# A two-block token-routed FFN: the second layer of block 1 token-major, two experts side by side, x1 turned feature-major by VectorE blocks and an HBM scratch

## The reference

```python
def block_1(h, ids):                       # h = layernorm(x), ctx is Wg, Wu and Wd
    for e in range(4):
        z = h @ ctx[e].T
        y = (silu(z) * z) @ ctx[e].T       # g and u are the same product
        out = where(expert_of(ids) == e, y, out)
x1 = x + block_1(layernorm(x), ids)

def block_2(h):
    scores = sigmoid(h @ router_w.T)
    combine = normalised scores of the 4 best of scores + e_bias, else 0
    routed = sum over e of combine[:, e] * ((silu(h @ gate[e].T) * (h @ up[e].T)) @ down[e].T)
    return routed + shared_expert(h)
out = x1 + block_2(layernorm(x1))
```

## Time and profile before

| | us |
|---|---|
| median of 3 runs | 173.52 (173.36 to 174.03) |
| the profiled execution | 173.89 |
| its span | 171.8 |
| PE busy | 166.6 (97%) |
| DVE busy | 114.2 (66%) |
| ACT busy | 67.8 (39%) |
| POOL busy | 39.6 (23%) |
| TensorE clock granted | 1.0 (2.4 GHz) |

### The profile page before, as it was taken

How to read it: one execution, slowest core, us unless ns; L and a number is a source line. 1 busy time by engine, 2 the same in 40 slices (tenths; PEclk the granted TensorE clock), 3 DMA queues, 4 the chain that set the end, 5 groups by cost and what they waited for, 6 DMA issues and landing times.

```text
span 171.8 us, 2194 instructions
## 1 busy us (share of the span) xinstructions
PE 166.6 (97%) x728; PEld 130.6 (76%) x728; DVE 114.2 (66%) x230; ACT 67.8 (39%) x112; POOL 39.6 (23%) x37
## 2 busy tenths in 40 slices
PE   6989999999999999999999999999999999999992
PEld 2568888888877888788787778788787887878881
DVE  0779778888984988588688528964744444444452
ACT  2472520551258254824664593152212222223320
POOL 2593000698200025539385000000000000000000
PEclk9999999999999999999999999999999999999999
DMA  4999000176400036742111200043361211100003
GB/s 137 307 373 352 23 4 2 25 236 227 122 0 4 15 130 181 203 160 67 61 61 61 61 0 4 8 126 126 113 195 45 75 65 61 62 0 4 2 0 122
DMA packets 7971, 16.41 MB, mean 95 GB/s; under 512 B 1336, under 2 KB 2200, under 8 KB 7832
## 3 DMA queue, kind: packets, MB, share of 16 engines
q1 hardware_dynamic: 7960, 16.27, 29.0%
HBM read 15.08 MB, written 1.18 MB: 95 GB/s over the span
## 4 chain that ended last, share of the span: by engine, by line
PE 97%; ACT 0%; POOL 0%; DVE 0%; issue 0%; DVEq 0%; POOLq 0%
PE bank L853 26%; PE bank L913 14%; PE bank L911 13%; PE bank L912 13%; PE bank L931 7%; PE bank L934 7%; PE bank L932 7%; PE bank L943 4%; PE bank L820 2%; PE bank L907 1%; PE bank L908 1%; PE bank L832 1%; ACT xn_hi L433 0%; POOL warm L383 0%; DVE xt L732 0%
## 5 line engine op out<-in xcount | busy, mean ns | idle before, releaser
L913 PE MATMUL bank<-xn_lo,gu_hi 128*128 128x512 f32 (+1 forms) x104 | 41.0, 394 | 0.0
L911 PE MATMUL bank<-xn_hi,gu_lo 128*128 128x512 f32 x96 | 37.9, 395 | 0.0
L912 PE MATMUL bank<-xn_hi,gu_hi 128*128 128x512 f32 x96 | 37.8, 394 | 0.0
L501 ACT ACTIVATE h_hi<-hid 128x512 fp32r<-128x512 f32 (+1 forms) x26 | 16.4, 632 | 45.7 <-DVE hid L720 45.7
L725 DVE TENSOR_TENSOR h_lo<-hid,h_hi 128x512 fp32r<-128x512 f32 (+1 forms) x26 | 20.2, 778 | 15.6 <-ACT h_hi L501 15.6
L913 PEld LDWEIGHTS bank<-xn_lo,gu_hi 128*128 128x128 f32 (+1 forms) x104 | 19.4, 186 | 5.0
L491 ACT ACTIVATE act_sb<-bank 128x512 f32<-128x512 f32 (+1 forms) x26 | 15.4, 594 | 18.1 <-PE bank L913 18.0
L398 POOL TENSOR_TENSOR gu_lo<-stage,gu_hi 128x512 fp32r<-128x512 f32 x12 | 17.9, 1516 | 17.6 <-ACT gu_hi L426 17.6
L912 PEld LDWEIGHTS bank<-xn_hi,gu_hi 128*128 128x128 f32 x96 | 18.0, 187 | 4.4
L911 PEld LDWEIGHTS bank<-xn_hi,gu_lo 128*128 128x128 f32 x96 | 18.0, 187 | 4.4
L931 PE MATMUL bank<-h_hi,wd_lo 128*128 128x512 f32 (+1 forms) x52 | 20.6, 396 | 0.0
(11 more groups left out here) (76 smaller groups left out, 213.1 us busy)
## 6 DMA issues: line engine op xcount, KB each, us to landing
stage<-gu_d SPq DMA_DIRECT2D x6, 512.0 KB, 3.5
stage<-wd_d SPq DMA_DIRECT2D x3, 512.0 KB, 4.1
x<-comb_d SPq DMA_DIRECT2D x8, 192.0 KB, 2.7
ids<-comb_d SPq DMA_DIRECT2D x8, 192.0 KB, 3.0
stage<-ctx_d SPq DMA_DIRECT2D x4, 256.0 KB, 5.0
xt<-xt_d SPq DMA_DIRECT2D x1, 1024.0 KB, 10.3
x<-comb_d SPq DMA_DIRECT2D x8, 128.0 KB, 3.1
ids<-comb_d SPq DMA_DIRECT2D x8, 128.0 KB, 2.8
```

What stands on the lines that cost most here:

```text
L911: nc.tensor.matmul(out[:], gu_lo[:, cols], xn_hi[:, h, k], start=(k == 0), stop=False)
L912: nc.tensor.matmul(out[:], gu_hi[:, cols], xn_hi[:, h, k], start=False, stop=False)
L913: ins = nc.tensor.matmul(out[0:rows, :], gu_hi[:, wide], xn_lo[:, h, k], start=False, stop=(k == KC - 1))
```

## The change

**Layer 1 stays as it was**: four mixes of 24 matmuls, now numbered 0 to 3. **Layer 2 becomes eight tiles** of 128 tokens: the tokens' hidden rows are now the stationary operand, two experts' matrices side by side (2 x 256 columns) the moving one, so a tile is two banks of six matmuls. `first_z` and three picks of 128x256 (mask `owned`, one value for a partition, broadcast over the row) choose the expert, and x1 is added in `x`, token-major. The order on PE is mix 0, mix 1, mix 2, tiles 0 to 3, mix 3 (with the norm's transposes after its third expert), gate and up of item 0, tiles 4 to 7.

**Gone**: the 1 MB load of `xt`, both groups of x1 transposes on PE, ACT's copies of x1 (`copy_x1`), `add_block_1`.

**x1 feature-major for the output** is made in two steps. At the end of g = 5 and g = 11 (`X1_TURNS`) DVE turns 32x32 blocks of the half's four tiles from `x` into `xt` (`turn_x1`, four instructions). SP then writes them to the scratch `x1_d` in HBM in eight DMAs (`write_x1`) and, one item later, reads them back in one (`read_x1`). The host orders the tokens of `x` and of the ids to suit; the norm's second transposes write PSUM in runs of 32 columns.

**The norm of x1, first half**, is made in two groups of two tiles (`NORM_GROUPS`), each with its own power on POOL; DVE takes tiles 0 and 2. The spread buffers lie in `ids` and `ctx_lo` now. On ACT the high parts of pieces 4 and 5 stand ahead of `silu_z(2)`.

```diff
-        mixes = [(1, 0, 0), (1, 0, 1), (1, 1, 0), (2, 0, 0), (2, 0, 1), (1, 1, 1), (2, 1, 0), (2, 1, 1)]
+        mixes = [(0, 0), (0, 1), (1, 0), (1, 1)]
+        units = [("mix", 0), ("mix", 1), ("mix", 2)] + [("tile", j) for j in range(TT)]
+        units += [("mix", 3)] + [("tile", j) for j in range(TT, HALVES * TT)]
...
+            def tile(j, masked):
+
+                u = ("tile", j)
+                z = prod[:, turn[u] % 2, 0:D]
+                dve.wait_ge(z_first, turn[u] + 1)
+                dve.wait_ge(dstep, masked)
+                for e in range(1, E1):
+                    dve.wait_ge(z_done, z_at[u, e // 2])
+                    if e > 1:
+                        dve.wait_ge(z_picked, picks_of(u, e - 1))
+                    nc.vector.copy_predicated(z, owned[:, e - 1, j:j + 1].to_broadcast([P, D]),
+                                              ring_bank(u, e // 2)[:, e % 2 * D:(e % 2 + 1) * D]).then_inc(z_picked, 1)
+                dve.wait_ge(z_picked, picks_of(u, E1 - 1))
+                nc.vector.tensor_tensor(x[:, j], z, x[:, j], ALU.add).then_inc(x1_done, 1)
+
+            def turn_x1(h):
+
+                for t in range(TT):
+                    nc.vector.transpose(x1_blocks[h][:, t], x[:, h * TT + t].rearrange("p (b i) -> p b i", i=LANES)).then_inc(x1_turned, 1)
...
+            def write_x1(h):
+                sp.wait_ge(x1_turned, (h + 1) * TT)
+                by_block = x1_d[h].rearrange("(b j) (q c) -> b q j c", b=BLOCKS, c=P)
+                blocks = xt[:, h].rearrange("p k c -> p (k c)")
+                for b in range(BLOCKS):
+                    sp.dma_start(by_block[b], blocks[:, b * P:(b + 1) * P]).then_inc(x1_out, 16)
+
+            def read_x1(h):
+                sp.wait_ge(x1_out, (h + 1) * BLOCKS * 16)
+                sp.dma_start(xt[:, h], x1_d[h].rearrange("(k f) c -> f k c", k=KC)).then_inc(xt_in, 16)
...
+                if g in X1_TURNS:
+                    write_x1(X1_TURNS.index(g))
+                if g - 1 in X1_TURNS:
+                    read_x1(X1_TURNS.index(g - 1))
...
-            first_z(2)
-            silu_z(2)
-            first_z(3)
+            first_z(("mix", 2))
             high_part(4)
             high_part(5)
+            silu_z(2)
...
-            rstd_of(2, 4)
+            rstd_of(3)
+            low_part(E1 + 2)
+            low_part(E1 + 3)
+            rstd_of(4)
...
+            def tile(j):
+
+                u = ("tile", j)
+                h, t = j // TT, j % TT
+                tokens = slice(t * P, (t + 1) * P)
+                for pair in range(E1 // 2):
+                    wait_ring_read(pe, u, pair)
+                    z = ring_bank(u, pair)[:]
+                    experts = slice(2 * pair, 2 * pair + 2)
+                    for k in range(KC):
+                        b = h * KC + k
+                        pe.wait_ge(h1_high, b + 1)
+                        nc.tensor.matmul(z, h_hi[:, b, tokens], ctx_hi[:, experts, k], start=(k == 0), stop=False)
```

More of the change, by code:

```diff
@@ L195, in build @@
[L195 to L211 removed]
+                      ("n2", 0, 0, 4), ("n2", 0, 1, 5), ("n2", 1, 0, 4), ("n2", 1, 1, 5)]
@@ new lines, in build, with banks_of @@
+        side_at = {u[:3]: n for n, u in enumerate(side_order)}
+        mixes = [(0, 0), (0, 1), (1, 0), (1, 1)]
+        units = [("mix", 0), ("mix", 1), ("mix", 2)] + [("tile", j) for j in range(TT)]
+        units += [("mix", 3)] + [("tile", j) for j in range(TT, HALVES * TT)]
+        turn = {u: n for n, u in enumerate(units)}
+        def banks_of(u):
+            return E1 if u[0] == "mix" else E1 // 2
+        z_at, ring_order = {}, []
+        for u in units:
+            for b in range(banks_of(u)):
+                z_at[u, b] = len(z_at) + 1
+                ring_order.append((u, b))
+            if u == ("mix", 3):
+                ring_order += [(("gate", 0), 0), (("up", 0), 0)]
@@ new lines, in build, with ring_bank, picks_of, wait_bank_picked @@
+        cycled = ring_order.index((("tile", HALVES * TT - 2), 0))
+        ring_banks = [first_ring[n % len(first_ring)] for n in range(cycled)] + [4, 5, 6, 7]
+        ring_at = {u: n for n, u in enumerate(ring_order)}
+        def ring_bank(u, b):
+            return bank[ring_banks[ring_at[u, b]]]
+        def picks_of(u, e):
+            return turn[u] * (E1 - 1) + e
+        def wait_bank_picked(eng, u, b):
+            if u[0] == "tile":
+                eng.wait_ge(z_picked, picks_of(u, 1 if b == 0 else E1 - 1))
+            elif b == 0:
+                eng.wait_ge(z_first, turn[u] + 1)
+            else:
+                eng.wait_ge(z_picked, picks_of(u, b))
@@ L612, in thresholds, with owners, pick @@
                 return last
-            def pick(n, masked, experts=range(1, E1)):
-                h = mixes[n][1]
-                dve.wait_ge(z_first, n + 1)
+            def owners():
+                dve.wait_ge(owner_in, 16)
+                for e in range(1, E1):
+                    last = step(nc.vector.tensor_scalar(owned[:, e - 1], owner[:], float(e * PER_EXPERT), None, ALU.is_ge))
+                return last
+            def pick(b, masked, experts=range(1, E1)):
+                u = ("mix", b)
+                h, _ = mixes[b]
+                dve.wait_ge(z_first, turn[u] + 1)
@@ L836, in mix @@
-            def mix(n, between={}, experts=range(E1), features=range(KC)):
-                layer, h, m = mixes[n]
-                f = slice(m * P, (m + 1) * P)
-                if layer == 1:
-                    parts = [(xn_hi[:, h, k], xn_lo[:, h, k]) for k in range(KC)]
-                else:
-                    parts = [(h_hi[:, h * KC + k], h_lo[:, h * KC + k]) for k in range(KC)]
-                def operands(k, low):
-                    if layer == 1:
-                        pe.wait_ge(xlo_done if low else xhi_done, h * KC + k + 1)
-                    else:
-                        pe.wait_ge(h1_done if low else h1_high, h * KC + k + 1)
-                def term(e, k, a, b, start=False, stop=False):
-                    return nc.tensor.matmul(ring_bank("z", n, e)[:], (ctx_hi, ctx_lo)[a][:, e, k, f], parts[k][b],
-                                            start=start, stop=stop)
-                for e in experts:
-                    if n == 0:
-                        pe.wait_ge(w_hi, e + 1)
-                    if 0 in features:
-                        wait_ring_read(pe, "z", n, e)
-                    for k in features:
+            def mix(b, between={}):
+                u = ("mix", b)
+                h, m = mixes[b]
+                f = slice(m * P, (m + 1) * P)
+                for e in range(E1):
+                    if b == 0:
+                        pe.wait_ge(w_hi, e + 1)
+                    wait_ring_read(pe, u, e)
+                    z = ring_bank(u, e)[:]
+                    for k in range(KC):
@@ L886, in gate_or_up @@
                 if g == 0:
-                    wait_ring_read(pe, "up" if up else "gate", 0, 0)
-                elif g == 1 and not up:
-                    pe.wait_ge(z_first, len(mixes))
+                    wait_ring_read(pe, ("up" if up else "gate", 0), 0)
                 elif g == 1:
-                    pe.wait_ge(z_picked, (len(mixes) - 1) * (E1 - 1) + 1)
+                    wait_bank_picked(pe, ("tile", TT), up)
                 elif up:
```

349 lines of the change are left out of this document (165 added, 184 removed).

## The result

The changed kernel takes **198.93 us** (197.34 to 200.68, 4 runs) beside 173.78 us of the kernel before (173.36 to 174.16) on the same chip: ratio 1.1417, 95% interval 1.1341 to 1.1494. The forecast was slower, 189, range 179 to 197: right in direction, 10 us too small, and outside its range. The ratio is that of the three faster executions (197.34, 198.88 and 198.98 us) and leaves out the slowest, 200.68. The profiled execution has a span of 195.6 us, 23.8 more than before.

What follows compares the result with a forecast made beforehand. PE bounds the kernel (97% busy), so only its instructions and new stops move the end. Transposes -1.75 and stops +5.0, +5.7 and +6.4 sum to +15.35 us on 173.89: forecast 189 us, range 179 to 197.

Steps and rivals of the forecast that it cites:

- The round trip is hidden: Rival "faster": PE is two items behind DVE, so x1's trip through HBM costs nothing; 171.8 us, chance 0.05.
- cheap writes: Rival: eight x1 writes issue at 0.30 us each, second and third stop lose 2.5 each; 184 us, chance 0.14.
- 16 transposes gone: PE loses the two groups of x1 transposes, 0.88 and 0.87 us: -1.75 us.
- first stop: PE waits at the norm's transposes of tile 3 in mix 3 for DVE's late norm: +5.0 us (3 to 7.5).
- turn of x1: DVE's four block transposes of 256 columns at the end of g = 5 take 1.5 us in all.
- eight issues: SP's eight x1 writes to HBM take 0.61 us each to issue, 4.9 us, ahead of item 6's spread rows.
- two spread issues and landing: Behind the x1 writes, two spread issues at 0.5 us and 2.3 us of landing delay DVE's product: 3.3 us.
- room from DVE's turn to PE's due time: Second stop: DVE ends g = 5 at 84.5, up(8) starts at 91.42; third: 4.7 us from g = 11's end.
- second stop: Item 5: PE waits 4.2 us at up(8) behind SP's x1 writes, then 1.5 at gate(9); together +5.7 (2.5 to 8).
- third stop: Item 11: PE waits at up(14) behind SP's x1 writes, with less room: +6.4 us (3.5 to 8).
- Sum: Whole kernel: -1.75 + 5.0 + 5.7 + 6.4 = +15.35 us on 173.89 gives 189.2, forecast 189.
- A gain is excluded, since the work is the same: Layer 2 on PE: 96 matmuls of the same size before and after, so their time changes by 0, no gain.

Runs made afterwards that it cites:

- e1: The changed kernel with SP issuing the eight writes of x1 four items later, all transfers and DVE work kept: 176.89 us, ratio 1.0182.
- e14: The changed kernel with each half of x1 written in four DMAs of 32 partitions instead of eight, run for its trace: 190.37 us.
- e6: The kernel before with PE held twice until POOL had done 7 memsets, two stops of 4.2 us: 186.65 us, ratio 1.0764.
- e7: The kernel before with PE held twice until POOL had done 12 memsets, two stops of 7.1 us: 192.70 us, ratio 1.1083.
- e8: The kernel before with 64 unused bytes a partition behind beyond, moving xn and h operands, no instruction changed: 170.54 us, ratio 0.9816.
- e5: The kernel before with PE held twice until POOL had done 3 memsets, two stops of 1.9 us: 178.31 us, ratio 1.0278.

## Why the prediction was right or wrong

**The places, and SP's queue: right.** The waits stand at the norm's transposes, at up(8) and at up(14), released by xn and by hid, with DVE idle 9.3 and 9.1 us for a spread DMA; e1 removed the second and third by SP's order alone. "The round trip is hidden" and "cheap writes" fall: the eight writes took 0.57 us each. The rule of the Trainium skill weighed ahead of the result ("DMA: Bandwidth & Descriptors", "Issuing engines are not separate DMA queues") would have put them near nothing; here initiating eight took 4.57 us beside 3.7 us until the next transfer had landed, and e14 shows that halving their number shortens each hole by about 3 us. The measurement decides.

**The terms, against the trace of after:**

| term | forecast | measured |
|---|---|---|
| 16 transposes gone | -1.75 | they are gone; their time has no row of its own |
| first stop | +5.0 | +4.8, 0.8 and 0.5 |
| turn of x1 | 1.5 | 1.41 |
| eight issues | 4.9 | 4.57 and 4.58 |
| two spread issues and landing | 3.3 | 4.7 and 4.5 |
| product and hid | 1.4 | 1.4 |
| room from DVE's turn to PE's due time, second stop | 6.9 | 6.4 |
| the same, third stop | 4.7 | 3.5 |
| second stop | +4.2 and 1.5 | +5.9 and 0.4 |
| third stop | +6.4 | +8.5 |
| matmuls at the lower clock | 0 | +6 |
| pitch of the matmuls | 0 | -3 to -4 |

**The step that failed** is the one that kept the pitch of the earlier trace rows for all matmuls: "Sum" adds the stops and the transposes to 173.89 and nothing else. Two terms are missing from it. The clock is the larger: +6 us by the count of matmuls at 0.427, and e6 and e7 have 2.4 us on average for a stop of such length. The placement of operands took 3 to 4 us off again: 3.1 by e8, or 660 x 0.0063 = 4.2 by the pitch. "A gain is excluded, since the work is the same" was wrong: the work was the same, and each matmul came 3% sooner. That the two errors partly cancel is luck.

**Mis-sized terms.** Landing: 2.3 us was read where the DMA engines had little to do (busy share 0.05 to 0.23 from 60 to 62 us of before; the earlier trace rows has the landing); behind eight writes of 64 KB it was 3.7 and 3.3, with a share of 0.77 from 97 to 102 us of after. That the writes themselves made it longer was not tested. The room between DVE's turn and PE's due time was read from before and was 0.5 and 1.2 us smaller in after; no experiment followed up why. Less 0.4 for turn and issues, these make up 1.5 and 2.0 of the 1.7 and 2.1 us by which the second and third stop were forecast too small.

**The sum.** Stops 21.0, slow matmuls 6, transposes -1.75, pitch -3.1 give +22.2; the spans differ by 23.8. About 1.6 us are not assigned to a row. Part may be the half microsecond that e5 shows beyond each stop.

**The first stop was right in its main cause, and in size partly by luck.** The forecast built it from DVE's sum of work, 2.5 us a tile (measured 2.4 without the waits) with hits by POOL. From the picks of mix 2 to the second variance, 30.1 to 48.3 us of after, DVE stands still for only 2.0 us: 0.97, 0.51 and 0.52 for ACT's copies at tiles 0, 1 and 3. The forecast had 1.1 and 0.6 for the first and last, and nothing for tile 1, where the two `prod` buffers made it wait. POOL's hits were too small: the masks, three int32 instructions, took 3.27 us, 2.2 more than alone, and h_lo ahead of them 0.8 more, where the forecast had 1.7 for both. So PE's last transposes could start at 49.6 instead of 48.9; but PE also came to them at 44.8 instead of 43.9, after two waits that the forecast did not have (0.5 and 0.8). The two misses cancel in the 4.8 us.

**The second half of the second stop** (gate(9), 1.5 forecast) was 0.4 in after, because PE itself ran slowly ahead of it; in e14, where only six of the twelve matmuls did, it was 1.66.
